# Attention stages with small heads: three stack buffers, stacks made in the third key tile, maxima in the first three key tiles, and maxima that alternate the 64-row halves

## The chip, the core and the metric

The kernel runs on one core of a Trainium2 chip. The metric is the device time of one execution in microseconds (us). Engines are named as in the profile: PE (TensorE), its weight loads PEld, DVE (VectorE), ACT (ScalarE), POOL (GpSimd), SP (the engine that issues the DMAs).

## The reference

The reference is a model of nine stages in float32 on x of 4 sequences of 512 tokens with 256 features: a selective-scan block, a mixture of experts, attention with rotary positions, experts, a gated pair of attentions ("pattern" and "latent"), experts, grouped attention, experts. The change is in three of the attentions, all softmax attention over 512 keys with very small heads:

```
# rotary (16 heads of width 16), queries and keys turned and normalised
logits = einsum('bhqd,bhkd->bhqk', qn, kn) / sqrt(16)
att = softmax(logits);  a = einsum('bhqk,bhkd->bhqd', att, v);  out = a @ Wo + bo
# pattern (16 heads of width 16), out is scaled by a gate
p_scores = einsum('bhqd,bhkd->bhqk', pq, pk) * 16 ** -0.5
# grouped (4 query groups x 8 heads of width 8, keys and values shared by the 4)
scores = einsum('bsqhd,bthd->bqhst', qh, kh) * scale
```

Every query row's maximum is subtracted before the exponential, as in the usual softmax.

## The kernel before

The stages run one after the other, and each of the three has a `Heads` object that writes one list of events. All engines walk this one list in its order and execute their share of it; semaphores order them against each other. So the list sets the order on every engine.

The unit of work is a group: four heads of one sequence. Rotary and pattern have 16 groups each (four to a sequence), grouped has 32 (eight to a sequence). In a group the keys come in four tiles of 128 (`kt` 0 to 3). For each key tile and each of its four heads PE makes a score matmul (event "s", 128 keys x 512 queries, line 1090), ACT takes its exponential into `probs` (line 1126), and PE multiplies probabilities and values in four matmuls of 32 columns each (event "pv", line 1096). The "pv" of a key tile stands after the four scores of the next one. The scores use three PSUM banks, so the score n waits for the exponential n - 3.

While group g runs, group g + 1 is prepared:

- Stacks ("ek", "eq", lines 1077 and 1078): a selection matrix times the high and the low half of projected keys or queries; ACT copies the result out as `k_stack` (line 1111) and `q_stack` (line 1115). In rotary and pattern a stack tile holds two heads, each in 64 of the 128 rows, and a group has two key and two query stacks. In grouped a group has one query stack (32 rows to a head), and the keys stand alone in `k_alone` (zeroes in the rows of the other heads), made once for eight groups. The stacks of g + 2 are made in group g and have two buffers.
- Maxima ("mx", line 1081 on PE, line 1149 on DVE): 16 for a group (four heads, four tiles of 128 queries). PE makes the scores of 128 queries against 512 keys, DVE reduces them to one column of `max_cols`. A maximum needs the stacks of its group.
- Bias (line 1086 on PE, line 1155 on DVE): four small matmuls turn the columns of maxima, DVE adds them to a row of `q_stack`. The first score of a group waits for it. Rotary and pattern have two (tiles 0 and 1), grouped has one.
- Norm ("norm", lines 1160 to 1171 on DVE): divides the sums of the group before, in the second key tile.

Each key tile has three slots in which prepared work stands: slots 0, 3, 6, 9 between its scores 0, 1 and 2 (half of a slot's events after score 0, half after score 1), slots 1, 4, 7, 10 the same around scores 2 and 3, slots 2, 5, 8, 11 after "pv". `schedule` (line 991) puts one maximum in slot 0, then 3, 3, 2, 2, 2 and 3 in slots 1, 3, 4, 6, 7 and 9, so the key tiles get 4, 5, 4 and 3. The bias of tile 0 stands in slot 5, the last bias in slot 10 (after the maxima of the fourth key tile), the stacks of g + 2 in slot 11, the last one of the group. In these slots stand as well the projections of the next sequence (means, "qk", "v", rotation), the normalisation of x, and the output projection ("out") of the last one; in rotary POOL cuts the turned heads of the next sequence into halves ("heads") in slot 3 of a sequence's third group and slot 6 of its fourth.

Everything on PE that is not a score or "pv" shares four PSUM banks in turn (`AUXB`, line 928): such an event waits until the reader (DVE or ACT) of the fourth event before it is done (`free`, line 1034).

## Time and profile before

| | us |
|---|---|
| median of three runs | 4568.15 |
| lowest, highest | 4564.28, 4572.83 |
| profiled execution, its time | 4568.12 |
| its span | 4566.3 |
| loop over groups: rotary, pattern, grouped | 389, 367, 633 |

The granted TensorE clock is 0.912 of full speed on the mean. A row of the profile gives an engine's busy time; "idle before" is how long the engine stood still before an instruction, and the name behind the arrow is what released it.

### The profile page before, as it was taken

How to read it: one execution, taken by the hardware profiler on the slowest of the kernel's cores; microseconds unless marked ns; L12 is line 12 of the kernel's file. 1: busy time of each engine (PE TensorE's matmuls, PEld its weight loads, DVE VectorE, ACT ScalarE, POOL GpSimd, SP SyncE). 2: the span in 40 equal slices, each digit the busy share in tenths (PEclk: the TensorE clock that was granted, in tenths of full speed). 3: DMA queues.
4: the chain of work that ended last, by engine and by line, in shares of the span. 5: the costliest groups of instructions: out<-in, count | busy, mean ns of one | idle time of the engine just before them, and what ended most of it. 6: DMA issues, size and time to landing. Idle time of an engine off the chain costs nothing.

```text
span 4566.3 us, 44420 instructions
## 1 busy us (share of the span) xinstructions
PE 3840.6 (84%) x15840; PEld 2548.4 (56%) x15840; DVE 2580.8 (57%) x4324; ACT 1687.5 (37%) x2807; POOL 1353.1 (30%) x1074
## 2 busy tenths in 40 slices
PE   6869778887978883888889887999878888879999
PEld 4647544435844432555555555788744444457887
DVE  5645366654456652678686765433356766655333
ACT  2433256653235540232323223222245555522222
POOL 3234322214320102333323314444322221143442
PEclk8989889988989976999999998999989999979999
DMA  1010000001000002101000101000000000010000
GB/s 56 1 37 5 29 1 1 1 1 41 1 22 5 5 5 80 28 16 26 18 24 17 26 16 58 18 27 9 16 1 1 1 1 1 1 58 21 25 13 19
DMA packets 32760, 83.27 MB, mean 18 GB/s; under 512 B 6304, under 2 KB 7456, under 8 KB 32288
## 3 DMA queue, kind: packets, MB, share of 16 engines
q1 hardware_dynamic: 32544, 80.44, 5.7%
q8 instruction: 130, 2.13, 0.2%
q14 instruction: 86, 0.70, 0.0%
HBM read 59.44 MB, written 4.19 MB: 14 GB/s over the span
## 4 chain that ended last, share of the span: by engine, by line
PE 54%; DVE 22%; ACT 5%; POOL 3%; issue 2%; DMA 1%; SPq 1%; DVEq 0%; POOLq 0%; ACTq 0%
PE ps L226 11%; PE ps L227 10%; PE ps L228 10%; DVE max_cols L1149 7%; PE ps L1096 5%; PE ps L1935 3%; PE ps L1090 2%; PE ps L296 2%; DVE q_lo L2112 2%; DVE max_cols L2128 2%; PE ps L1081 2%; ACT probs L1126 1%; PE ps L1086 1%; PE ps L800 1%; PE ps L1077 1%
## 5 line engine op out<-in xcount | busy, mean ns | idle before, releaser
L1149 DVE TENSOR_REDUCE max_cols<-ps 128x1 fp32r<-128x512 f32 x1024 | 635.6, 680 | 284.9 <-PE ps L1081 284.1
L1126 ACT ACTIVATE probs<-ps 128x512 f32<-128x512 f32 x1024 | 546.1, 603 | 256.5 <-PE ps L1090 164.6
L754 POOL TENSOR_TENSOR h_lo<-h,h_hi 128x512 fp32r<-128x512 f32 x304 | 392.5, 1291 | 816.6 <-ACT h_hi L834 816.6
L911 DVE TENSOR_TENSOR gated<-silu,ps 128x512 f32<-128x512 f32 x288 | 197.9, 687 | 689.1 <-PE ps L228 665.7
L828 ACT ACTIVATE silu<-ps 128x512 f32<-128x512 f32 x304 | 181.9, 598 | 928.0 <-PE ps L228 927.9
L226 PE MATMUL ps<-xn_hi,w_hi 128*128 128x512 f32 x1216 | 479.5, 394 | 0.0
L227 PE MATMUL ps<-xn_lo,w_hi 128*128 128x512 f32 x1216 | 476.0, 391 | 0.0
L228 PE MATMUL ps<-xn_hi,w_lo 128*128 128x512 f32 x1216 | 475.8, 391 | 0.0
L1096 PE MATMUL ps<-probs,v_aug 128*32 128x512 f32 x2048 | 310.3, 683 | 0.0
L330 POOL CAST o_hi<-o_scaled 128x512 fp32r<-128x512 f32 x64 | 39.1, 612 | 910.1 <-DVE o_scaled L1171 910.1
L1935 PE MATMUL ps<-probs,v_tok 128*128 128x512 f32 x512 | 263.5, 611 | 2.7 <-ACT denominators L1997 2.7
L226 PEld LDWEIGHTS ps<-xn_hi,w_hi 128*128 128x128 f32 x1216 | 231.0, 190 | 49.8 <-issue 1.0
L227 PEld LDWEIGHTS ps<-xn_lo,w_hi 128*128 128x128 f32 x1216 | 230.4, 189 | 49.6 <-issue 1.4
L228 PEld LDWEIGHTS ps<-xn_hi,w_lo 128*128 128x128 f32 x1216 | 230.0, 189 | 48.6
L226 PE MATMUL ps<-h_hi,w_hi 128*128 128x512 f32 x608 | 249.4, 410 | 1.2 <-POOL h_lo L754 1.2
L1090 PE MATMUL ps<-q_stack,k_alone 128*128 128x512 f32 x512 | 213.9, 440 | 31.3 <-ACT probs L1126 29.1
L227 PE MATMUL ps<-h_lo,w_hi 128*128 128x512 f32 x608 | 239.7, 394 | 0.0
L228 PE MATMUL ps<-h_hi,w_lo 128*128 128x512 f32 x608 | 239.6, 394 | 0.0
L1090 PE MATMUL ps<-q_stack,k_stack 64*128 64x512 f32 x512 | 198.8, 485 | 43.3 <-ACT probs L1126 41.2
L1987 ACT ACTIVATE probs<-ps 128x1024 f32<-128x1024 f32 x128 | 131.2, 1025 | 279.1 <-PE ps L1932 278.9
L1081 PE MATMUL ps<-k_alone,q_stack 128*128 128x512 f32 x512 | 201.7, 432 | 37.8 <-ACT q_stack L1115 23.7
L2128 DVE TENSOR_REDUCE max_cols<-ps 128x1 fp32r<-128x512 f32 x256 | 169.2, 682 | 89.6 <-PE ps L1921 89.3
(460 smaller groups left out, 7896.1 us busy)
## 6 DMA issues: line engine op xcount, KB each, us to landing
raw<-in_w_ffn SPq DMA_DIRECT2D x76, 448.0 KB, 3.3
raw<-raw SPq DMA_DIRECT2D x256, 64.0 KB, 2.0
composed_inputs<-in_m_latent SPq DMA_DIRECT2D x1, 5120.0 KB, 15.5
raw<-in_w_mamba SPq DMA_DIRECT2D x8, 448.0 KB, 5.9
raw<-in_w_latent SPq DMA_DIRECT2D x5, 448.0 KB, 16.8
x<-in_x SPq DMA_DIRECT2D x4, 512.0 KB, 6.2
gated_pattern<-gated SPq DMA_DIRECT2D x4, 512.0 KB, 3.1
raw<-gated_pattern SPq DMA_DIRECT2D x4, 512.0 KB, 4.3
```

What stands on the lines that cost most here:

```text
L226: nc.tensor.matmul(psum, wh, xh, start=start, stop=False)
L227: nc.tensor.matmul(psum, wh, xl, start=False, stop=False)
L228: return nc.tensor.matmul(psum, wl, xh, start=False, stop=stop)
L754: nc.gpsimd.tensor_tensor(HL[:, b % 3, :], hb[:, b % 2, :], HH[:, b % 3, :].bitcast(F32), ALU.subtract).then_inc(G.sem, G.step((s, ev)))
L911: nc.vector.tensor_tensor(ga if routed(i) else hb[:, i % 2, :], sg[:, i % 2, :], bank[2 + i % 2], ALU.mult).then_inc(V.sem, V.step((s, "ga ...
L1081: last = nc.tensor.matmul(self.psum(ev), self.q_rows(g, h)[:, q * P:(q + 1) * P], self.k_rows(g, h), start=True, stop=True)
L1090: last = nc.tensor.matmul(self.scores(self.step_no(g, kt, h)), self.k_rows(g, h)[:, kt * P:(kt + 1) * P], self.q_rows(g, h), start=True, s ...
L1096: last = nc.tensor.matmul(bank[6][32 * h:32 * h + 32, :], self.VA[:, (g // self.G4) % 2, kt, self.khead((g % self.G4) * 4 + h), :], self.P ...
L1126: nc.scalar.activation(self.PB[:, n % 8, :], self.scores(n), ACT.Exp, scale=self.scale).then_inc(A.sem, A.step((s, ("exp", n))))
L1149: nc.vector.tensor_reduce(self.MB[:, self.tile_of(g, h) % 2, q, col:col + 1], self.psum(ev), op=ALU.max, axis=AX.X, negate=True).then_inc( ...
L1935: last = nc.tensor.matmul(bank[6 + i], VT[:, (g // HP) % 2, kt, 64 - 64 * i:192 - 64 * i], PB[:, (g * QT + kt) % 2, i, :], start=kt == 0, ...
L2128: nc.vector.tensor_reduce(MB[:, q, 32 * i:32 * i + 1], bank[slot(ev)], op=ALU.max, axis=AX.X, negate=True).then_inc(V.sem, V.step((s, ev)))
```

## The change

- `q_stack` and `k_stack` get three buffers, indexed by g % 3.
- The stacks of g + 2 stand in slot 8 (after "pv" of the third key tile) and no longer in slot 11.
- The maxima of g + 1 are dealt by a table, in halves of a key tile: 2, 2 | 4, 2 | 4, 2 | 0, 0. The key tiles get 4, 6, 6 and 0.
- In rotary and pattern all maxima of a half stand between its two scores, and of each pair of heads the one in the upper 64 rows comes first. The list then reads lower, upper, lower, upper half ... from score 0 to score 1, and again from score 2 to 3. In grouped half of the maxima stand between the two scores and half behind the second.
- What else is in a slot comes whole after its second score; it is no longer split around it.

The biases stay in slots 5 and 10, "norm" in slot 4.

```diff
+        FIRST_MX = (0, 2, 4, 8, 10, 14, 16, 16, 16)
...
-                self.QS = alloc("q_stack", [P, 2, self.tiles, L], F32R)
-                self.KS = None if k_tiles else alloc("k_stack", [P, 2, self.tiles, L], F32R)
+                self.QS = alloc("q_stack", [P, 3, self.tiles, L], F32R)
+                self.KS = None if k_tiles else alloc("k_stack", [P, 3, self.tiles, L], F32R)
...
             def maxima(self, g):
-                return [("mx", g, t * self.per + i, q) for t in range(self.tiles) for q in range(QT) for i in range(self.per)]
+                turn = range(self.per) if self.k_tiles else (1, 0)
+                return [("mx", g, t * self.per + i, q) for t in range(self.tiles) for q in range(QT) for i in turn]
...
                     if n < self.NG:
-                        mx, had = self.maxima(n), 0
-                        for pos, count in ((0, 1), (1, 3), (3, 3), (4, 2), (6, 2), (7, 2), (9, 3)):
-                            self.slots[g][pos] = mx[had:had + count] + self.slots[g][pos]
-                            had += count
...
                     if g + 2 < self.NG:
-                        self.slots[g][11] = self.stacks(g + 2) + self.slots[g][11]
+                        self.slots[g][8] = self.stacks(g + 2) + self.slots[g][8]
...
-                    for h in range(4):
-                        if n < len(units):
-                            events.append(("s",) + units[n] + (h,))
-                        here = at[h // 2]
-                        events += here[len(here) // 2:] if h % 2 else here[:len(here) // 2]
+                    for k in range(2) if n < len(units) else ():
+                        g, kt = units[n]
+                        one, two = (("s", g, kt, h) for h in (2 * k, 2 * k + 1))
+                        mx = self.maxima(g + 1)[FIRST_MX[2 * kt + k]:FIRST_MX[2 * kt + k + 1]] if g + 1 < self.NG else []
+                        if self.k_tiles:
+                            events += [one] + mx[:len(mx) // 2] + [two] + mx[len(mx) // 2:] + at[k]
+                        else:
+                            events += [one] + mx + [two] + at[k]
```

PE in the pattern stage, before, from the fourth key tile of its fourteenth group to the start of the next group (q_stack<- and k_stack operands side by side are scores in line 1090 and maxima in line 1081; 1086 is the bias, 1096 "pv", 1077 and 1078 the stacks):

```order
L1090 MATMUL ps<-q_stack,k_stack 128x512
L1081 MATMUL ps<-k_stack,q_stack 128x512
L1090 MATMUL ps<-q_stack,k_stack 128x512
L1081 MATMUL ps<-k_stack,q_stack 128x512 x2
L1090 MATMUL ps<-q_stack,k_stack 128x512 x2
L1086 MATMUL ps<-h_pattern_hi,max_cols 128x128 x4
L1096 MATMUL ps<-probs,v_aug 32x512 x4
L1077 MATMUL ps<-heads_hi,h_pattern_hi 128x512
L1078 MATMUL ps<-heads_lo,h_pattern_hi 128x512
...
L1090 MATMUL ps<-q_stack,k_stack 128x512 x2
L1081 MATMUL ps<-k_stack,q_stack 128x512
```

PE at the same place now (each line number is one higher), from the third key tile to the start of the next group:

```order
L1091 MATMUL ps<-q_stack,k_stack 128x512 x2
L1082 MATMUL ps<-k_stack,q_stack 128x512 x2
L1091 MATMUL ps<-q_stack,k_stack 128x512
L1097 MATMUL ps<-probs,v_aug 32x512 x4
L1078 MATMUL ps<-heads_hi,h_pattern_hi 128x512
L1079 MATMUL ps<-heads_lo,h_pattern_hi 128x512
...
L1091 MATMUL ps<-q_stack,k_stack 128x512 x4
L1087 MATMUL ps<-h_pattern_hi,max_cols 128x128 x4
L1097 MATMUL ps<-probs,v_aug 32x512 x4
L1091 MATMUL ps<-q_stack,k_stack 128x512
L1082 MATMUL ps<-k_stack,q_stack 128x512 x2
```

The stacks stood between the last "pv" of a group and the next group's first score; now they stand before the four scores of the fourth key tile, and the maxima of that key tile are gone from it.

PE in the grouped stage, before, from the fourth key tile of a plain group to the next group's first scores:

```order
L1090 MATMUL ps<-q_stack,k_alone 128x512
L1081 MATMUL ps<-k_alone,q_stack 128x512
L1090 MATMUL ps<-q_stack,k_alone 128x512
L1081 MATMUL ps<-k_alone,q_stack 128x512 x2
L1090 MATMUL ps<-q_stack,k_alone 128x512 x2
L1086 MATMUL ps<-h_grouped_hi,max_cols 128x128 x4
L1096 MATMUL ps<-probs,v_aug 32x512 x4
L1077 MATMUL ps<-heads_hi,h_grouped_hi 128x512
L1078 MATMUL ps<-heads_lo,h_grouped_hi 128x512
L1090 MATMUL ps<-q_stack,k_alone 128x512 x2
```

PE at the same place now, from the "pv" in the third key tile to the next group's first maximum:

```order
L1097 MATMUL ps<-probs,v_aug 32x512 x4
L1078 MATMUL ps<-heads_hi,h_grouped_hi 128x512
L1079 MATMUL ps<-heads_lo,h_grouped_hi 128x512
L1091 MATMUL ps<-q_stack,k_alone 128x512 x4
L1087 MATMUL ps<-h_grouped_hi,max_cols 128x128 x4
L1097 MATMUL ps<-probs,v_aug 32x512 x4
L1091 MATMUL ps<-q_stack,k_alone 128x512
L1082 MATMUL ps<-k_alone,q_stack 128x512
```

The four scores of the fourth key tile now follow each other with no maximum between them, and the one stack stands ahead of them.

## Rows read from the trace of the kernel before

**Rows 1.** The profile's first part: busy time, share of the span, instructions.
```profile
PE 3840.6 (84%) x15840; PEld 2548.4 (56%) x15840; DVE 2580.8 (57%) x4324; ACT 1687.5 (37%) x2807; POOL 1353.1 (30%) x1074
```

**Rows 2.** Loops: us, busy PE, PEld, DVE, ACT, POOL, PEclk, DMA, GB/s.
```profile
616.00:1005.00 389.00, 332.60 (x1501) 162.23 (x1500) 259.71 (x433) 239.16 (x421) 84.23 (x76) 0.92 0.00 1
1331.00:1698.00 367.00, 312.92 (x1482) 153.64 (x1481) 227.45 (x381) 196.41 (x367) 38.62 (x36) 0.89 0.01 5
3354.00:3987.00 633.00, 534.25 (x2457) 274.61 (x2455) 428.80 (x722) 354.97 (x651) 126.75 (x111) 0.94 0.00 1
```

**Rows 3.** Waits of DVE, rotary, pattern, grouped loop: us, times, longest.
```profile
DVE max_cols L1149 <- PE ps L1081: 66.9, 28, 5.4
...
DVE max_cols L1149 <- PE ps L1081: 67.9, 23, 4.8
...
DVE max_cols L1149 <- PE ps L1081: 129.3, 77, 8.1
DVE q_stack L1155 <- PE ps L1086: 25.0, 28, 4.0
```

**Rows 4.** DVE, timeline, pattern: start, us, operation, [idle before it and what ended it].
```profile
1638.48 0.69 DVE L1155 TENSOR_TENSOR q_stack<-q_stack,ps 128x512 fp32r<-128x512 f32 x1 [0.75 <-PE ps L1086]
1642.21 2.57 DVE L1149 TENSOR_REDUCE max_cols<-ps 128x1 fp32r<-128x512 f32 x4 [3.04 <-PE ps L1081]
...
1657.87 1.89 DVE L1149 TENSOR_REDUCE max_cols<-ps 128x1 fp32r<-128x512 f32 x3 [1.17 <-PE ps L1081]
...
1666.41 2.48 DVE L1149 TENSOR_REDUCE max_cols<-ps 128x1 fp32r<-128x512 f32 x4 [4.76 <-PE ps L1081]
```

**Rows 5.** Timeline of PE, pattern stage, one group's end and the next one's start.
```profile
1637.78 0.66 PE L1086 MATMUL ps<-h_pattern_hi,max_cols 128*128 128x128 f32 x4 [1.03 <-DVE max_cols L1149]
1638.38 1.06 PE L1096 MATMUL ps<-probs,v_aug 128*32 128x512 f32 x8
1639.37 0.50 PE L1077 MATMUL ps<-heads_hi,h_pattern_hi 128*128 128x512 f32 x1
...
1642.92 0.50 PE L1090 MATMUL ps<-q_stack,k_stack 64*128 64x512 f32 x1 [0.51 <-ACT probs L1126]
...
1655.14 1.93 PE L1096 MATMUL ps<-probs,v_aug 128*32 128x512 f32 x8
```

**Rows 6.** Timeline of ACT over the same boundary.
```profile
1640.14 0.69 ACT L1111 ACTIVATE k_stack<-ps,c 128x512 fp32r<-128x512 f32 x1 [2.48 <-PE ps L1078]
...
1642.25 2.08 ACT L1126 ACTIVATE probs<-ps 128x512 f32<-128x512 f32 x4
```

**Rows 7.** Timeline of DVE, grouped stage, first maxima of three groups.
```profile
3507.98 0.69 DVE L1149 TENSOR_REDUCE max_cols<-ps 128x1 fp32r<-128x512 f32 x1 [7.80 <-PE ps L1081]
...
3713.18 2.48 DVE L1149 TENSOR_REDUCE max_cols<-ps 128x1 fp32r<-128x512 f32 x4 [1.12 <-PE ps L1081]
...
3731.18 2.48 DVE L1149 TENSOR_REDUCE max_cols<-ps 128x1 fp32r<-128x512 f32 x4 [2.15 <-PE ps L1081]
```

**Rows 8.** Timeline of PE and ACT, grouped stage, one boundary.
```profile
3727.64 0.66 PE L1086 MATMUL ps<-h_grouped_hi,max_cols 128*128 128x128 f32 x4 [1.38 <-DVE max_cols L1149]
...
3729.23 0.51 PE L1077 MATMUL ps<-heads_hi,h_grouped_hi 128*128 128x512 f32 x1
...
3730.49 2.06 ACT L1126 ACTIVATE probs<-ps 128x512 f32<-128x512 f32 x4
```

**Rows 9.** Busy time by stretch, pattern stage, same columns as group 2.
```profile
1655.00:1664.00 9.00, 8.47 (x31) 3.54 (x31) 4.27 (x7) 2.09 (x5) 0.76 (x1) 0.50 0.01 2
```

**Rows 10.** Timeline of PE, rotary stage: one score and one maximum matmul.
```profile
735.95 0.50 PE L1090 MATMUL ps<-q_stack,k_stack 64*128 64x512 f32 x1
735.95 0.49 PE L1081 MATMUL ps<-k_stack,q_stack 64*128 64x512 f32 x1
```

**Rows 11.** Timeline of POOL and PE, rotary stage, the third group of a batch.
```profile
684.15 1.28 POOL L332 TENSOR_TENSOR heads_lo<-rotated,heads_hi 128x512 fp32r<-128x512 f32 x1
...
688.24 1.06 PE L1096 MATMUL ps<-probs,v_aug 128*32 128x512 f32 x8
```

More of the change, by code:

```diff
@@ L980, in k_rows @@
                     return self.KZ[:, (g // self.G4) % 2, self.khead((g % self.G4) * 4 + h), :]
-                return self.KS[r, g % 2, h // self.per, :]
+                return self.KS[r, g % 3, h // self.per, :]
             def q_rows(self, g, h):
                 r = slice((h % self.per) * self.rows, (h % self.per + 1) * self.rows)
-                return self.QS[:, g % 2, h // self.per, :] if self.k_tiles else self.QS[r, g % 2, h // self.per, :]
+                return self.QS[:, g % 3, h // self.per, :] if self.k_tiles else self.QS[r, g % 3, h // self.per, :]
             def k_tile_no(self, g, h):
@@ L1109, in act @@
                         r = slice(i * self.rows, (i + 1) * self.rows) if self.k_tiles else slice(0, P)
-                        to = self.KZ[r, (g // self.G4) % 2, t * self.per + i, :] if self.k_tiles else self.KS[:, g % 2, t, :]
+                        to = self.KZ[r, (g // self.G4) % 2, t * self.per + i, :] if self.k_tiles else self.KS[:, g % 3, t, :]
                         nc.scalar.activation(to, self.psum(ev)[r, :], ACT.Identity, bias=self.one[r, :]).then_inc(A.sem, A.step((s, ev)))
@@ L1114, in act @@
                     act.wait_ge(PE.sem, PE.at((s, ev)))
-                    nc.scalar.activation(self.QS[:, g % 2, t, :], self.psum(ev), ACT.Copy).then_inc(A.sem, A.step((s, ev)))
+                    nc.scalar.activation(self.QS[:, g % 3, t, :], self.psum(ev), ACT.Copy).then_inc(A.sem, A.step((s, ev)))
                 elif kind == "v":
@@ L1152, in vec @@
                     g, t = ev[1:]
-                    q = self.QS[:, g % 2, t, :]
+                    q = self.QS[:, g % 3, t, :]
                     dve.wait_ge(PE.sem, PE.at((s, ev)))
```

## The prediction

> **What bounds the kernel now.** I read the profile from coarse to fine: the busy shares, the stretches of the three loops that the change touches, the waits of DVE in each of them, then the timelines around one end of a group.
>
> No engine is full. PE is busy for 84% of the span and DVE for 57% [rows 1]. In the loops DVE works 260 of 389, 227 of 367 and 429 of 633 us, so it stands still for 129, 140 and 204 us [rows 2]. What it stands still for is mostly the first maximum of something: 66.9, 67.9 and 129.3 us before line 1149, each time waiting for PE [rows 3]. Two thirds of busy time on an engine, with waits in one place, is the picture of a chain that goes from engine to engine. The timelines show it.
>
> In pattern the last maximum of a group ends, PE makes the bias matmuls, having waited 1.03 us for DVE [rows 5], and DVE adds the bias after 0.75 us [rows 4]. Then PE does "pv", which takes 1.0 us to the start of the stacks, and the eight stack matmuls [rows 5], ACT copies the four stacks out in 2.1 us [rows 6], and only behind this stands the first maximum of the next group: DVE has waited 3.04 us in one group and 4.76 us in the next [rows 4]. In the second of them PE was at half its clock: the same "pv" takes 1.93 us and not 1.06 [rows 5], and the stretch has a granted clock of 0.50, which is 1.2 GHz [rows 9]. In grouped the same wait is 2.15 us with one stack in it, 7.80 us where the keys of the next sequence are stacked as well, and 1.12 us where no stack came between [rows 7]; PE itself waits 1.38 us for the last maximum before the bias [rows 8].
>
> So once in a group first PE waits for DVE's queue of maxima, and then DVE waits for PE and ACT to make stacks. The change puts the stacks over the queue.
>
> **The sum, by DVE's waits.** DVE's own work is the same before and after (as many maxima, adds and norms; a third buffer costs SBUF and no time). So I price the change by what DVE stands still for in a group.
>
> *The gap after the last bias.* Rotary and pattern have 14 ends of a group each in which stacks are made and maxima follow, 28 in all. The gap is 3.9 us, the mean of the 3.04 and the 4.76 [rows 4]; 28 of them are 109 us of the 134.8 us [rows 3]. With the stacks gone from it, it is the one without a stack, 1.12 us [rows 7]. Saved: 2.8 us each, 78 us.
>
> *The new wait before the last bias.* The fourth key tile has no maxima now. From the last maximum's matmul PE has to do: the second score beside it, 0.2 (an estimate, under half of a matmul's 0.50 [rows 10], since matmuls overlap), "pv" 1.0, stacks and scores up to the last score 3.55 (1639.37 to 1642.92, in which that score waits for ACT's copies and first exponential), to the bias 0.3 and the bias 0.66 [rows 5]. That is 5.7 us. DVE has work for a part of it: PE can be at most four maxima ahead, since they share four banks, and four take 2.48 us [rows 4]. DVE waits 3.2 us where it waits 0.75 now [rows 4], 2.5 us more. 28 of them are 70 us, so of the 78 only 8 are left. This is the core of my forecast: most of the wait is not removed but moved to the other side of the bias.
>
> *What fills the new wait.* In the first group of each later sequence (3 in rotary, 3 in pattern) the normalisation of x stands in slot 9, in the fourth key tile: by the code two multiplies and one or two transposes on DVE, at about 0.7 us each like the add of the bias [rows 4] some 2.5 us. It now runs in the new wait: 6 x 2.5 = 15 us.
>
> *The late maxima.* In the fourth key tile DVE waits for PE to hand it the last three maxima, 1.17 us in the group shown [rows 4]. Of the 134.8 us [rows 3] 26 are not in the gaps; I take half, 13 us, for this and count it as saved, because in the second and third key tile the maxima come four at a time and DVE has a queue.
>
> Rotary and pattern together: 8 + 15 + 13 = 36 us.
>
> *Grouped.* 28 plain ends: the gap goes from 2.15 to 1.12 us [rows 7], 1.0 saved. The path before the bias: 0.2 + 1.0 + 1.9 (stack at 3729.23, ACT's exponentials from 3730.49, the first 0.6 long [rows 8]) + 0.3 + 0.66 = 4.1 us less 2.48 of queue is 1.6, and 0.75 now: 0.8 lost. Left: 28 x 0.2 = 6 us. At the three ends with key stacks (7.80 us [rows 7]) the extra 5.65 us of ACT copies moves in front of the bias whole: saved 3 x 6.7 = 20, lost 3 x (4.1 + 5.65 - 2.48 - 0.75) = 3 x 6.5 = 20, nothing left. The rest of the 129.3 us is 129.3 - 28 x 2.15 - 3 x 7.8 = 46 us; a quarter, 11 us, for late maxima (the queue is thinner here, the three maxima were spread between scores), and 2 us for the normalisation in slot 9. Grouped: 19 us.
>
> Sum: 36 + 19 = 55 us. PE's own wait before the bias (1.03 and 1.38 us [rows 5, 8]) isn't counted beside it: it is the same end of a group seen from PE, while DVE works.
>
> *Edits at nothing.* Slot 4 holds the norm and now six maxima share its key tile: DVE gets behind, PE stops at a bank of the four, and the score behind it waits too. That costs nothing while DVE is what is waited for, and it is why I take nothing for PE's waits there; between none and what the slower rival below takes. Rotary's stacks now come one key tile earlier and could wait for POOL's cut of the heads. In the third group of a sequence the cut ends at 685.43 (684.15 + 1.28), and slot 8 begins at the end of the "pv" at 689.24 [rows 11]: 3.8 us to spare, at three places; if the cover were gone it would cost at most some us each. Whole slots behind the second score in place of halves move an event by a matmul or two: nothing, from -3 to +3 us.
>
> *The halves.* A score and a maximum in opposite halves of rows start together at 735.95 [rows 10], so the array runs both. Counting runs of alternating halves, two to a place, a group takes 5 + 5 + 4 + 4 = 18 places before and 4 + 5 + 5 + 2 = 16 now. Two places of at most 0.5 us in 31 groups bound it at 31 us; none excludes zero. I take zero, since in the key tiles where the pairs gain PE then waits for a bank that DVE has not read. The Trainium skill, "TensorEngine Tiling (Array Packing)", section "PSUM Bottleneck", says the same from the other side: tiles speed up TensorE but not the reading of PSUM, which may become the bottleneck. By that rule the halves give 0, by PE alone up to 31 us.
>
> The profiled execution took 4568.12 us (1.8 over its span), the median is 4568.15, so no correction: 4568.1 - 55 = **4513 us**.
>
> **Rivals.**
>
> *A. The wait only moves.* The fills and late maxima are my estimates (28 and 13 us); without them 14 us stay, and three or four waits for banks in groups with other work take these. For it: the 78 against the 70. Against: PE's wait for the last maximum does vanish. Time about 4565 us, within 9 us (0.2%, what a measurement of this kernel can tell) of no change.
>
> *B. The gap counts in full.* If PE and ACT and not DVE set the pace in most groups (other work of 3 us and more stands in them, PE is busy 85% [rows 2]), DVE's new wait in the fourth key tile is hidden, and the saving is the gap: 78 in rotary and pattern, 28 + 20 in grouped, 126 us. For it: PE's busy share. Against: much of that is 1.2 GHz time and overlap. Time: 4442 us.
>
> *C. Slower, through the clock.* The second and third key tile are now bound by DVE: six maxima, the norm, a bias, while PE has little and stands at banks. If the granted clock falls there to 1.2 GHz, as in [rows 9] after such waits, PE is slow just when it makes the path to the bias: of the 4.7 us that are PE's own work in it (all but about 1 us of ACT) almost as much again (1.93 for 1.06 [rows 5]), 4.2, less 1.5 that hides behind ACT, and 1.5 in the gap: 4 us an end. The saving is 55 / 59 = 0.9 us an end, so it decides from 14 of 59 ends that are slow and weren't. With 20: 80 - 55, 4593 us. The clock is 0.92, 0.89 and 0.94 now [rows 2]; it needs to fall by 0.05 or so. The Trainium skill, "TensorE: Matmul & The Clock Gate", Part 1, has the clock follow how busy PE has been of late; the trace agrees as far as it goes (0.50 in [rows 9]).
>
> *D. The halves do what they can.* It adds up to 31 us to my forecast: 4482 us, inside my range.
>
> **How the numbers follow.** Forecast with D 0.56 (its own range 4480 to 4552), B 0.17, A 0.14, C 0.13. Faster by over 0.2%: 0.56 + 0.17 and a little of A, 0.74; within 0.2%: 0.14; slower: 0.12. The range goes from B's 4442 to just before A's far side, 4566.
>
> **What would show it.** After the last bias DVE's wait is 1.1 us in all three stages; before the last bias it is about 3 us in rotary and pattern and 1.6 in grouped, over 6 where keys are stacked. PE's wait for DVE before line 1087 is near zero, and new waits of PE before line 1082 for DVE appear in the second and third key tile. The granted clock of the loops stays within 0.03. I am wrong if the wait before the bias is far below 3 us (then B), if the clock falls (C), or if the loops save under 10 us together although the gap is 1.1 us (A).

## The result, and the profile after

| | before | after |
|---|---|---|
| median of five runs each, us | 4568.15 | 4587.12 |
| lowest to highest | 4564.28 to 4572.83 | 4579.73 to 4594.83 |
| profiled execution, its span | 4568.12, 4566.3 | 4579.73, 4577.9 |
| mean granted clock | 0.912 | 0.910 |

The ratio is 1.0039, with a 95% interval of 1.0023 to 1.0055. The change makes the kernel 19 us slower. I forecast 4513 us, 55 us faster, with a range from 4442 to 4566 us; the result is outside it.

The first part of the page hardly moves (after; as [rows 1]):

```profile
PE 3847.8 (84%) x15840; PEld 2554.4 (56%) x15840; DVE 2572.9 (56%) x4324; ACT 1699.4 (37%) x2807; POOL 1353.5 (30%) x1074
```

The loops say where the time went. To compare like with like I cut each from its first "pv" to its last. Columns as in [rows 2]; rotary, pattern, grouped. Before:

```profile
625.00:1021.00 396.00, 340.01 (x1532) 163.01 (x1535) 257.67 (x431) 242.18 (x429) 86.12 (x78) 0.91 0.00 1
1337.00:1699.00 362.00, 308.74 (x1467) 151.53 (x1470) 222.89 (x374) 193.02 (x360) 38.62 (x36) 0.89 0.01 5
3364.00:3988.00 624.00, 525.39 (x2434) 269.19 (x2437) 421.58 (x711) 349.86 (x643) 126.75 (x111) 0.95 0.00 1
```

After:

```profile
626.00:1042.00 416.00, 352.54 (x1530) 166.36 (x1526) 253.63 (x429) 245.68 (x428) 86.08 (x78) 0.87 0.00 1
1357.00:1713.00 356.00, 304.54 (x1466) 149.60 (x1468) 220.44 (x373) 196.05 (x359) 38.55 (x36) 0.90 0.01 5
3376.00:4003.00 627.00, 525.78 (x2434) 272.27 (x2436) 420.36 (x710) 353.01 (x642) 126.89 (x111) 0.94 0.00 1
```

Rotary is 20 us longer (21 to a tenth: 395.4 and 416.3), pattern 6 shorter, grouped 3 longer. DVE's busy time in each is 1 to 4 us shorter than before, so what was added is waiting. The three loops together are 18 us longer, everything outside them 6 us shorter, which gives the 11.6 us between the two profiled executions. The medians are 19 us apart.

DVE around the last bias (after; line 1156 is its bias add, 1150 its maxima): rotary, pattern twice, the grouped group in which keys are stacked, and a plain grouped one.

```profile
903.75 0.69 DVE L1156 TENSOR_TENSOR q_stack<-q_stack,ps 128x512 fp32r<-128x512 f32 x1 [3.75 <-PE ps L1087]
...
1640.23 0.69 DVE L1156 TENSOR_TENSOR q_stack<-q_stack,ps 128x512 fp32r<-128x512 f32 x1 [6.51 <-PE ps L1087]
...
1662.31 0.69 DVE L1156 TENSOR_TENSOR q_stack<-q_stack,ps 128x512 fp32r<-128x512 f32 x1 [1.43 <-PE ps L1087]
1663.77 2.48 DVE L1150 TENSOR_REDUCE max_cols<-ps 128x1 fp32r<-128x512 f32 x4 [0.77 <-PE ps L1082]
...
3519.91 0.69 DVE L1156 TENSOR_TENSOR q_stack<-q_stack,ps 128x512 fp32r<-128x512 f32 x1 [9.06 <-PE ps L1087]
...
3747.07 0.69 DVE L1156 TENSOR_TENSOR q_stack<-q_stack,ps 128x512 fp32r<-128x512 f32 x1 [1.99 <-PE ps L1087]
3748.72 2.48 DVE L1150 TENSOR_REDUCE max_cols<-ps 128x1 fp32r<-128x512 f32 x4 [0.96 <-PE ps L1082]
```

The wait after the bias, 3.04 and 4.76 us before [rows 4], is 0.77; the wait ahead of it, 0.75 before, is 1.4 to 6.5 in these rows, and 9 where keys are stacked. The stacks have carried their wait to the other side of the bias. (Before, the longest wait ahead of a bias was 1.2 us in rotary and pattern and 4.0 us in grouped.)

Now everything else that DVE waits for. Waits of DVE (us in total, times, longest) in the rotary loop, before:

```profile
DVE max_cols L1149 <- PE ps L1081: 62.3, 26, 5.4
...
DVE z L1429 <- PE ps L1295: 14.4, 12, 3.2
DVE x L1439 <- PE ps L228: 13.1, 6, 3.8
DVE q_stack L1155 <- PE ps L1086: 10.2, 13, 1.1
```

and after:

```profile
DVE q_stack L1156 <- PE ps L1087: 55.9, 12, 8.6
DVE z L1430 <- PE ps L1296: 26.5, 12, 4.4
DVE x L1440 <- PE ps L228: 23.1, 6, 6.5
...
DVE max_cols L1150 <- PE ps L1082: 12.3, 8, 3.7
```

The maxima wait 50.0 us less, the bias 45.7 us more. The reads of the next sequence's rotation (`z`) and of the last one's output projection (`x`) wait 12.1 and 10.0 us more. These four rows give 18 of the 21 us. In pattern it is the same: maxima 54.5 less, bias 28.9 more, and `heads_lo` and `gated` 24.4 more:

```profile
DVE q_stack L1156 <- PE ps L1087: 39.3, 13, 6.5
DVE heads_lo L1616 <- ACT heads_hi L1567: 37.8, 12, 5.0
DVE gated L1622 <- PE ps L228: 23.8, 6, 5.7
DVE max_cols L1150 <- PE ps L1082: 10.4, 12, 1.9
```

(before, the same stretch of the loop:)

```profile
DVE max_cols L1149 <- PE ps L1081: 64.9, 22, 4.8
DVE heads_lo L1615 <- ACT heads_hi L1566: 21.7, 11, 2.5
DVE gated L1621 <- PE ps L228: 15.5, 6, 3.8
DVE q_stack L1155 <- PE ps L1086: 10.4, 13, 1.2
```

One place shows how. DVE after, in a rotary group; the `z` transposes read what PE makes in the slots of the other work:

```profile
895.80 1.28 DVE L1150 TENSOR_REDUCE max_cols<-ps 128x1 fp32r<-128x512 f32 x2
899.28 0.72 DVE L1430 STREAM_TRANSPOSE z<-ps 128x512 f32<-128x512 f32 x1 [2.21 <-PE ps L1296]
903.75 0.69 DVE L1156 TENSOR_TENSOR q_stack<-q_stack,ps 128x512 fp32r<-128x512 f32 x1 [3.75 <-PE ps L1087]
```

Its last two maxima end at 897.08. Then PE makes four stacks and the rotation's matmuls, DVE waits 2.21 us for them, does 0.72 us of work, and waits 3.75 us more. The edit writes `self.stacks(g + 2) + self.slots[g][8]`, so the eight stack matmuls stand ahead of everything else in slot 8. PE at this place, after (1078 is a stack matmul, 1296 the one that `z` reads):

```profile
896.26 0.50 PE L1078 MATMUL ps<-heads_hi,h_rotary_hi 128*128 128x512 f32 x1
...
898.22 1.02 PE L1296 MATMUL ps<-raw,c 128*128 128x512 f32 x2
```

So the stacks take 1.96 us of PE in front of it. The same `z` read before the change, when no stack stood there:

```profile
883.12 0.72 DVE L1429 STREAM_TRANSPOSE z<-ps 128x512 f32<-128x512 f32 x1 [0.31 <-PE ps L1295]
```

In grouped the two waits of the core alone are DVE's balance (before 127.4 and 23.8 in this stretch; after, here):

```profile
DVE q_stack L1156 <- PE ps L1087: 77.4, 28, 9.1
DVE max_cols L1150 <- PE ps L1082: 70.1, 60, 3.4
```

57.3 saved and 53.6 lost.

### The profile page after: what moved, and what is told of

Its sections match the earlier page's. It is cut to its first block, busy times and chain, and to the rows that moved or that the text cites. A ratio compares the mean times of both kernels' runs of the same rounds, so it can differ in the third digit from the quotient of the medians.

```text
span 4577.9 us, 44488 instructions
## 1 busy us (share of the span) xinstructions
PE 3847.8 (84%) x15840; PEld 2554.4 (56%) x15840; DVE 2572.9 (56%) x4324; ACT 1699.4 (37%) x2807; POOL 1353.5 (30%) x1074
## 4 chain that ended last, share of the span: by engine, by line
PE 56%; DVE 20%; ACT 5%; POOL 3%; issue 2%; DMA 1%; SPq 1%; DVEq 0%; POOLq 0%; ACTq 0%
PE ps L226 10%; PE ps L227 10%; PE ps L228 10%; PE ps L1097 5%; DVE max_cols L1150 5%; PE ps L1091 3%; PE ps L1082 3%; PE ps L1936 3%; PE ps L296 2%; DVE max_cols L2129 2%; DVE q_lo L2113 2%; ACT probs L1127 1%; PE ps L800 1%; PE ps L1078 1%; PE ps L1922 1%
## 5 line engine op out<-in xcount | busy, mean ns | idle before, releaser
L1150 DVE TENSOR_REDUCE max_cols<-ps 128x1 fp32r<-128x512 f32 x1024 | 629.5, 679 | 124.2 <-PE ps L1082 118.2
L1127 ACT ACTIVATE probs<-ps 128x512 f32<-128x512 f32 x1024 | 556.4, 601 | 378.8 <-PE ps L1091 283.2
L1082 PE MATMUL ps<-k_stack,q_stack 64*128 64x512 f32 x512 | 194.5, 488 | 73.0 <-DVE q_stack L1156 42.0
L1082 PE MATMUL ps<-k_alone,q_stack 128*128 128x512 f32 x512 | 205.5, 440 | 50.3 <-DVE max_cols L1150 25.9
```

Of the source, the lines that this page charges most:

```text
L1082: last = nc.tensor.matmul(self.psum(ev), self.q_rows(g, h)[:, q * P:(q + 1) * P], self.k_rows(g, h), start=True, stop=True)
L1127: nc.scalar.activation(self.PB[:, n % 8, :], self.scores(n), ACT.Exp, scale=self.scale).then_inc(A.sem, A.step((s, ("exp", n))))
L1150: nc.vector.tensor_reduce(self.MB[:, self.tile_of(g, h) % 2, q, col:col + 1], self.psum(ev), op=ALU.max, axis=AX.X, negate=True).then_inc( ...
```

## The experiments

Two theories stood from the start. In the first, DVE's order costs the time: the maxima are bunched in the first three key tiles and the fourth is empty. In the second, the granted clock costs it: the order lets PE stand still at places after which it gets 1.2 GHz. Each kernel was timed in five rounds against the kernel before. The table holds what all of them gave; a loop's product of time and clock counts each us at half speed as half a us. The clock is the mean over forty equal stretches of the loop. The product is a diagnostic, not a law: a wait for an engine other than PE does not get shorter with PE's clock.

| kernel | ratio to before, 95% | rotary: us, clock, product | pattern | grouped |
|---|---|---|---|---|
| before | | 395, .909, 359 | 362, .887, 321 | 624, .945, 590 |
| after | 1.0039, 1.0023 to 1.0055 | 416, .874, 364 | 356, .905, 322 | 626, .937, 587 |
| e1_stacks_only | 0.9985, 0.9970 to 0.9999 | 411, .875, 360 | 366, .873, 319 | 600, .949, 569 |
| e2_maxima_only | 1.0075, 1.0052 to 1.0098 | 411, .888, 365 | 364, .878, 320 | 641, .933, 598 |
| e3_rotary_as_before | 1.0012, 0.9994 to 1.0030 | 392, .918, 360 | 352, .918, 323 | 630, .932, 587 |
| e4_maxima_even | 1.0052, 1.0033 to 1.0071 | 408, .885, 361 | 365, .882, 322 | 624, .926, 578 |
| e5_stage_mix | 0.9943, 0.9929 to 0.9958 | 396, .912, 361 | 356, .905, 322 | 600, .949, 570 |
| e6_after_filled | 1.0036, 1.0022 to 1.0051 | 406, .928, 376 | 351, .928, 325 | 626, .937, 587 |
| e7_before_filled | 1.0003, 0.9990 to 1.0016 | 398, .919, 366 | 348, .946, 329 | 624, .943, 588 |
| e8_halves_and_whole_slots | 1.0105, 1.0090 to 1.0121 | 399, .911, 363 | 368, .873, 321 | 661, .914, 604 |
| e9_dealt_as_before | 0.9979, 0.9969 to 0.9990 | 404, .882, 356 | 349, .926, 323 | 603, .953, 575 |
| e10_mix_and_fill | 0.9934, 0.9921 to 0.9947 | 389, .929, 362 | 346, .951, 329 | 600, .949, 569 |
| e11_grouped_middle | 0.9969, 0.9957 to 0.9980 | 389, .930, 362 | 358, .900, 322 | 600, .963, 578 |

How far one trace can be trusted: where the same order stands in several kernels, its loop took 389 to 396 us (rotary as before, five traces), 352 to 358 (pattern as after, four), 626 to 630 (grouped as after, three), 600 each (grouped with before's dealing and slot 8, three). So 4 us either way are scatter.

**e1_stacks_only.** The kernel before, with three buffers and the stacks in slot 8.

```diff
-                self.QS = alloc("q_stack", [P, 2, self.tiles, L], F32R)
+                self.QS = alloc("q_stack", [P, 3, self.tiles, L], F32R)
...
-                        self.slots[g][11] = self.stacks(g + 2) + self.slots[g][11]
+                        self.slots[g][8] = self.stacks(g + 2) + self.slots[g][8]
```

> The kernel before with three stack buffers and the stacks in slot 8; the maxima stay at 4, 5, 4 and 3 to the key tiles, and slots are split in halves as before. Theory 1 (the dealing of the maxima, which leaves none in the fourth key tile, costs what the stacks' new place saves): faster than before, 4530 to 4550 us, with DVE's gap after the last bias near 1.1 us and its wait before the last bias under 1.5 us in most groups. Theory 2 (the stacks' new place itself costs, by ACT's copies standing before the fourth key tile's exponentials): 4568 us or more. Theory 3 (the granted clock is the cause and not a sign): the clock of the rotary loop decides whatever the order, 0.87 and about 4585 us if it falls, 0.91 and below 4568 us if not.

Measured: 4563.27 us, between the expectations: grouped saves 24 us, as the first theory has it; rotary loses 16 with its clock at 0.875, as the second and third have it; pattern loses 4, which is scatter. Waits of DVE in the grouped loop:

```profile
DVE max_cols L1149 <- PE ps L1081: 98.7, 80, 3.9
DVE q_stack L1155 <- PE ps L1086: 25.2, 27, 2.9
```

The maxima wait 28.7 us less than before and the bias only 1.4 us more (127.4 and 23.8 in the same stretch). With maxima still in the fourth key tile DVE has something to do while PE makes the stack, and the wait doesn't move but goes. In grouped this is what my forecast hoped for, and the stacks alone bring it.

In rotary and pattern e1 shows something else. Its maxima stand where they stood before, yet the reads that I found lengthened in the kernel after are as long here:

```profile
DVE x L1439 <- PE ps L228: 24.1, 6, 7.0
DVE z L1429 <- PE ps L1295: 21.0, 12, 2.2
...
DVE heads_lo L1615 <- ACT heads_hi L1566: 38.7, 12, 5.0
DVE gated L1621 <- PE ps L228: 23.4, 6, 5.8
```

There are 36 such reads in the two loops, and 18 of them stand in slot 8 (6 `z`, 3 `x`, 6 `heads_lo`, 3 `gated`). Their waits, added up over the timelines, in us:

| | before | e1 | e9 | e4 | after | e2 | e8 |
|---|---|---|---|---|---|---|---|
| stacks in slot | 11 | 8 | 8 | 8 | 8 | 11 | 11 |
| maxima to the key tiles | 4, 5, 4, 3 | 4, 5, 4, 3 | 4, 5, 4, 3 | 4, 4, 4, 4 | 4, 6, 6, 0 | 4, 6, 6, 0 | 4, 4, 4, 4 |
| the 18 reads in slot 8 | 26.5 | 68.9 | 66.4 | 66.2 | 79.0 | 39.4 | 25.4 |
| all 36 reads | 64.8 | 107.1 | 98.1 | 102.5 | 111.2 | 82.8 | 62.7 |

So it is mainly the stacks in front of these reads that lengthen them, 42 us with no maximum moved. Moving the maxima away adds about 10 to it (e1 and after), or 13 where the stacks stay in slot 11 (before and e2).

**e2_maxima_only.** The kernel after, with the stacks back in slot 11.

```diff
-                        self.slots[g][8] = self.stacks(g + 2) + self.slots[g][8]
+                        self.slots[g][11] = self.stacks(g + 2) + self.slots[g][11]
```

> The kernel after with the stacks back in slot 11; maxima dealt 4, 6, 6 and 0. Theory 1: slower than both kernels, 4600 us or more, since the wait of about 4 us behind the last bias is back and the empty fourth key tile stays. Theory 2: near or below before, about 4560 us.

Measured: 4603.43 us; grouped 641. Its waits there:

```profile
DVE max_cols L1150 <- PE ps L1082: 118.4, 64, 8.1
DVE q_stack L1156 <- PE ps L1087: 47.1, 28, 3.9
```

Bias 23 us more than before, maxima 9 less. The new dealing costs 17 us in grouped with the stacks in slot 11, and 26 with them in slot 8 (626 against e1's 600). In both pairs the half-slots differ too; e9 takes these out.

**e3_rotary_as_before.** The kernel after, with rotary's list as before (`self.old`: before's dealing and half-slots, stacks in slot 11).

```diff
+        OLD = (C_ROT,)
...
+                        if self.old:
+                            mx, had = self.maxima(n), 0
+                            for pos, count in ((0, 1), (1, 3), (3, 3), (4, 2), (6, 2), (7, 2), (9, 3)):
...
-                        self.slots[g][8] = self.stacks(g + 2) + self.slots[g][8]
+                        at_ = 11 if self.old else 8
+                        self.slots[g][at_] = self.stacks(g + 2) + self.slots[g][at_]
```

> The kernel after, but rotary keeps the order of before (its buffers are three). The traces put the loss of the change into rotary (its loop 404 us before, 424 after), with 4 us won in pattern and 4 lost in grouped. If that holds, this kernel takes 4568 minus 4 plus 4 minus about 3 between the stages, 4560 to 4570 us. If the loss of rotary comes from something outside its order (a placement of buffers, a clock that falls anyway), it stays at 4585 us.

Measured: 4575.16 us, rotary 392. That is above the 4560 to 4570 us expected, and by its ratio (1.0012) it can't be told from before. (The expectation cuts the rotary loop elsewhere; by the cut used here its 404 and 424 us are 395 and 416.) The loss is rotary's, and the stages can be changed apart from each other.

**e4_maxima_even.** The kernel after with four maxima in each key tile.

```diff
-        FIRST_MX = (0, 2, 4, 8, 10, 14, 16, 16, 16)
+        FIRST_MX = (0, 2, 4, 6, 8, 10, 12, 14, 16)
```

> The kernel after with the maxima dealt evenly, 4, 4, 4 and 4 to the key tiles, everything else as in it (stacks in slot 8, halves alternating, slots whole). Theory 1: the best so far, 4510 to 4545 us, since DVE has maxima queued while PE makes stacks and rotations, and the bias follows them closely. Theory 2: no better than after, 4585 us. If the whole slots behind the second score are what costs, also about 4585 us.

Measured: 4588.96 us, grouped 624, where 4510 to 4545 us were expected. Filling the fourth key tile to its end is no cure. The bias wait goes back (25.6 us), but now PE waits for the last maximum. Waits of PE in the grouped loop, e4:

```profile
PE ps L1087 <- DVE max_cols L1150: 45.1, 31, 3.7
```

and e1, whose last maxima stand behind score 1 and so two scores ahead of the bias:

```profile
PE ps L1086 <- DVE max_cols L1149: 23.1, 25, 1.4
```

So there is a best place for the last maxima, between the two ends. The first theory in its simple form (the more evenly dealt, the better) fell.

**e5_stage_mix.** Each stage in its best list so far: rotary as before, pattern as after, grouped with before's dealing and half-slots and stacks in slot 8.

```diff
+        OLD = (C_ROT, C_GRP)
...
+                        at_ = 11 if self.old and not self.k_tiles else 8
+                        self.slots[g][at_] = self.stacks(g + 2) + self.slots[g][at_]
```

> Rotary in the order of before, pattern in the order of after, grouped with the stacks in slot 8 but its maxima and slots as before. The stages are independent if the traces are read rightly: rotary 395, pattern 352 to 356, grouped 600 us against 395, 362 and 624 before, so 4568 - 0 - 8 - 24 = about 4536 us. If instead the loops' times only scatter with the granted clock and no order is better than another, it comes out at 4560 to 4575 us.

Measured: 4539.92 us; the three loops came as in the kernels that they are taken from, within 1 us.

**e6_after_filled.** The kernel after, with one score and one maximum of each rotary and pattern group written four times into the same bank: six matmuls more in a group, the same values.

```diff
+                    again = 4 if not self.k_tiles and ev == self.maxima(g)[12] else 1
+                    for _ in range(again):
...
+                    again = 4 if not self.k_tiles and (kt, h) == (3, 2) else 1
+                    for _ in range(again):
```

> The kernel after; in rotary and pattern the third score of the fourth key tile and the thirteenth maximum of a group are made four times over into the same bank (six more matmuls a group, the same values), at places where PE is about to wait. Theory 3 (half-clock time is the cause of rotary's loss): the mean clock of the rotary loop rises from 0.874 to 0.91 or more and the loop shortens by 8 us or more from 416 us although PE does some 20 us more work. Theory 1 (the waits themselves cost, and the clock only follows): the loop takes 416 us or more. Pattern likewise, from 356 us.

Measured: 4581.53 us. The loops (rotary, pattern):

```profile
628.00:1034.00 406.00, 351.45 (x1628) 175.91 (x1627) 254.22 (x429) 246.12 (x429) 86.08 (x78) 0.93 0.00 1
1351.00:1702.00 351.00, 313.06 (x1557) 164.56 (x1559) 220.61 (x372) 195.04 (x359) 38.57 (x36) 0.93 0.01 5
```

With 96 matmuls more the rotary loop takes 10.8 us less, PE's busy time is 1 us shorter, and the clock goes from 0.87 to 0.93. More work is not faster by itself, so this trace puts a part of rotary's time to the clock, as the second theory has it: about half of the 21 us come back. The timed runs don't confirm it: the ratios to before are 1.0036 and 1.0039, with overlapping intervals. The gain and its size rest on one trace. The order of the waits stays as after (bias 55.2, `z` 25.5, `x` 22.8 us).

**e7_before_filled.** The same with the kernel before (scores 2 of the first and 3 of the fourth key tile, four times).

```diff
+                    again = 4 if not self.k_tiles and (kt, h) in ((0, 2), (3, 3)) else 1
+                    for _ in range(again):
```

> The kernel before; in rotary and pattern the third score of the first key tile and the last score of the fourth are made four times over into the same bank, before the waits for ACT's exponential and for the last maximum. Theory 3: clock of rotary from 0.909 and of pattern from 0.887 up by 0.02 or more and both loops 4 us or more shorter (395 and 362 us now). Otherwise the loops stay or grow by up to 10 us each.

Measured: 4570.61 us. Rotary, pattern:

```profile
630.00:1028.00 398.00, 353.56 (x1624) 179.50 (x1620) 258.19 (x430) 242.79 (x428) 86.02 (x78) 0.92 0.00 1
1347.00:1695.00 348.00, 308.66 (x1558) 160.54 (x1562) 223.25 (x373) 192.42 (x359) 38.55 (x36) 0.95 0.01 5
```

Pattern is 14 us shorter at a clock of 0.95, rotary not shorter: its clock was 0.91 and had little to give. The timed ratio (1.0003) shows no gain of the whole; the pattern's rests on this trace, taken of one of the faster runs, and on e10's.

**e8_halves_and_whole_slots.** e4 with the stacks in slot 11: of the change, mainly the alternating halves and the whole slots are left.

```diff
-        FIRST_MX = (0, 2, 4, 8, 10, 14, 16, 16, 16)
+        FIRST_MX = (0, 2, 4, 6, 8, 10, 12, 14, 16)
...
-                        self.slots[g][8] = self.stacks(g + 2) + self.slots[g][8]
+                        self.slots[g][11] = self.stacks(g + 2) + self.slots[g][11]
```

> The kernel after with stacks in slot 11 and the maxima dealt 4, 4, 4 and 4: what is left of the change is the alternation of the halves, the whole slots behind the second score, and the third buffer. If the alternation pays, 4555 us or less. If the whole slots cost (the even dealing came to 4589 us where the stacks alone came to 4563), 4585 us or more. If neither matters, 4568 us, and the two parts of the change only hurt together.

Measured: 4614.97 us, the slowest. Rotary (399) and pattern (368) are about as before; the loss is in grouped:

```profile
3373.00:4034.00 661.00, 534.36 (x2431) 277.22 (x2430) 424.36 (x712) 344.78 (x641) 126.76 (x111) 0.91 0.00 1
```

Even dealing with late stacks has both waits: PE waits for the last maximum, then DVE for the stack. The gain of slot 8 over slot 11 at this dealing is 37 us, at before's 24, at after's 15. So the edits don't add, and e8 didn't isolate what it was made for.

**e9_dealt_as_before.** The kernel after with before's counts in each key tile, 4, 5, 4, 3: the halves and whole slots stay.

```diff
-        FIRST_MX = (0, 2, 4, 8, 10, 14, 16, 16, 16)
+        FIRST_MX = (0, 1, 4, 7, 9, 11, 13, 16, 16)
```

> The kernel after with the maxima dealt as before, 1, 3, 3, 2, 2, 2, 3 and 0 to the half key tiles; stacks in slot 8, slots whole behind the second score, upper half first. If the dealing is what costs in grouped (theory 1), its loop takes 595 to 605 us, as with the stacks alone and slots in halves (600), and not 626. If the whole slots cost, it stays at 620 us or more. Rotary stays near 410 us either way, since its stacks stand in slot 8. Whole kernel: 4565 or 4590 us.

Measured: 4551.95 us, below both values expected. Rotary and grouped:

```profile
628.00:1032.00 404.00, 346.84 (x1528) 172.01 (x1527) 256.62 (x430) 242.60 (x426) 86.02 (x78) 0.88 0.00 1
3368.00:3971.00 603.00, 512.28 (x2433) 269.45 (x2429) 422.68 (x710) 345.12 (x642) 126.90 (x111) 0.95 0.00 1
```

One table of numbers turns the whole from 1.0039 to 0.9979, and grouped from 626 to 603 us. Against e1, from which it differs by the halves and whole slots alone, grouped is equal within scatter. Pattern is 17 us shorter (366, 349), but its product is not (319, 323), and the ratios are the same, so this is no gain by places in the array. Rotary stays long (404), as its stacks stand in slot 8.

**e10_mix_and_fill.** e5 with pattern's list as before and e7's repeated scores in pattern alone.

```diff
+        OLD = (C_ROT, C_PAT, C_GRP)
...
+                    again = 4 if self.fill and (kt, h) in ((0, 2), (3, 3)) else 1
```

> Rotary in the order of before, grouped with only the stacks in slot 8, pattern in the order of before with the repeated scores (six more matmuls a group) that raised its clock. Theory 3 and the independence of stages: pattern's loop 348 us at a clock near 0.945, grouped 600, rotary 395; whole kernel 4540 - 8 = about 4530 us. If pattern's 348 us was chance, 4540 us or more.

Measured: 4527.42 us, ratio 0.9934, below before and after. It can't be told from e5 (0.9943): the intervals overlap. Pattern again takes 346 us at 0.95:

```profile
1336.00:1682.00 346.00, 306.82 (x1558) 159.60 (x1554) 223.10 (x373) 192.78 (x359) 38.62 (x36) 0.95 0.01 5
```

**e11_grouped_middle.** e5 with grouped's maxima dealt 4, 5, 5, 2.

```diff
-                            for pos, count in ((0, 1), (1, 3), (3, 3), (4, 2), (6, 2), (7, 2), (9, 3)):
+                            for pos, count in ((0, 1), (1, 3), (3, 3), (4, 2), (6, 3 if self.k_tiles else 2), (7, 2), (9, 2 if self.k_tiles else 3)):
```

> The stage mix (rotary as before, pattern as after) with grouped's maxima dealt 4, 5, 5 and 2. Theory 1, as the runs now leave it: PE's wait before the bias shrinks and DVE's wait there grows as maxima move out of the fourth key tile, with the best somewhere between; grouped's loop within 6 us of 600, against 600 at 4, 5, 4, 3 and 624 at 4, 4, 4, 4. A loop above 610 us would say that the place of single maxima against other work, and not their number in the last key tile, decides.

Measured: 4547.73 us, grouped 600 as with 4, 5, 4, 3. By the traces two or three maxima in the fourth key tile do equally well, and none costs 23 us. The timed runs are less kind to two: the ratio is 0.9969 against e5's 0.9943, and the intervals barely touch.

## Why the prediction was wrong

*The gap after the last bias: right.* I said 3.9 to 1.12 us, saved 78 us in rotary and pattern. The gaps, from the end of the last bias to the first maximum, added up over the timelines, went from 57 to 20 us in rotary and from 55 to 11 in pattern: 81 us. In grouped the maxima wait 57.3 us less, I had 60 with all terms.

*The path from the last maximum to the last bias: this step failed.* I built it from "pv", stacks, scores and bias, 5.7 us, with nothing else in slot 8, and I took DVE's other waits as unchanged without a reason. But in 12 of the 14 groups in which rotary and pattern make stacks, slot 8 holds other work of PE (rotation, projections, "out"), and the eight stack matmuls now stand ahead of it. Where DVE reads that work, it waits for the stacks there: the `z` and `x` reads of rotary wait 22.1 us more, `heads_lo` and `gated` of pattern 24.4. This term of 46.5 us is missing from my sum. In e1, where no maximum has moved, it is 42 us; the rest goes with the maxima that stood beside these reads. Where ACT reads the work (the values, fourth group of a sequence) the wait lands on the bias instead, as no maximum is left ahead of it: 6.5 us in pattern and 6.8 to 8.6 in rotary, where I had 3.2.

*The new wait before the last bias: right in place, too small in size.* I said 70 us less 15 for fills, 55, and it is 45.7 + 28.9 = 75 us. The fill itself came true: at five of the six ends with the normalisation of x in slot 9 the bias waits 0 us. At the others I had 3.2 everywhere, and they are 3.75 us at plain ends of rotary, 0.94 at plain ends of pattern (whose wait stands at `heads_lo`, ahead of it) and over 6 in the fourth groups. In grouped I had 42 and it is 53.6. At ends with key stacks it is 9 us, where I had over 6. The core of the forecast, that the wait moves to the other side of the bias, is what the trace shows.

*"The late maxima", 13 + 11 us saved: true as a wait, wrong as time.* In rotary and pattern the maxima wait 104.5 us less, 77 of it right at the end of the gaps, 27 elsewhere, more than my 13. It comes back at the bias and at the other reads. So rotary and pattern come out as -104.5 + 74.6 + 46.5, with 5 us of smaller rows and 6.5 us less work on DVE 15 us longer, where I had 36 shorter. In grouped the choice between dealing the maxima 4, 5, 4, 3 and 4, 6, 6, 0 is worth 23 us (e9 and after), and early stacks save 24 us where the former dealing stays (e1). They cancel: that is why grouped stands at 626 for 624, where I had 19 us saved.

*DVE's waits as the price: not enough in rotary and pattern.* A loop is DVE's work and its waits, so that account always closes; but how long it waits for PE hangs on PE's clock too, and I took that as given. The product of time and clock stays at 356 to 365 us in rotary in all eleven lists without repeated matmuls there, and at 319 to 323 in the ten such lists of pattern. Over these orders the loops' times differ mostly in how much of them runs at 1.2 GHz. In rotary this is 2 x (1 - 0.909) x 395 = 72 us before and 105 after; by this estimate half speed costs up to half of the 33, some 17 of the 21 us. Repeated matmuls raised the clock in the traces of e6 (rotary) and e7 (pattern), and those loops got shorter. The Trainium skill, "TensorE: Matmul & The Clock Gate", section "A second HAM failure mode: psum-queue depth-cycling", has a kernel in which short idle times between groups of matmuls let the clock swing between its two levels; e6 agrees as far as it goes, with 0.874 going to 0.928 for six matmuls more in a group. In grouped the product moves by 35 us with the order (569 to 604), and there DVE's waits were the better price.

*Edits at nothing.* Whole slots and alternating halves: nothing in grouped (600, 603) and none that the ratios show elsewhere. PE's waits for DVE in the second and third key tile came as foretold (25.9 us in grouped before line 1082), and cost nothing that I could set apart. POOL's cut of the heads, for which I had 3.8 us to spare in the third group of a sequence, held PE up in the fourth, which I had not looked at (rotary loop, after):

```profile
PE ps L1302 <- POOL heads_hi L330: 5.3, 3, 1.8
```

There ACT's copies of the stacks stand behind its own work on what POOL makes (ACT waits 3.30 us for it at 720.45), and PE waits for a bank that ACT has not read.

*The rivals.* A was the nearest in its mechanism: the wait moves and the small terms that I added are not there. It had no term for the other work and gave 4565. C gave 4593 with a chance of 0.13, the time nearest to the measured 4587, but that is partly luck. It named the clock, which fell by 0.035 in rotary, more than the 0.03 that I allowed, rose in pattern and fell by 0.008 in grouped. Its cause was six maxima to a key tile, and that is not it: e1 and e9 deal 4, 5, 4 and 3, and their rotary clock is 0.875 and 0.882. B and D are out: no hidden wait, no gain by halves.

*What stays open.* Why rotary's clock falls. All four lists with its stacks in slot 8 (after, e1, e4, e9) have it at 0.874 to 0.885, and the lists of before in slot 11 at 0.909 to 0.930; but e2 has 0.888 with slot 11 and e8 0.911. So it isn't the slot alone. PE's own waits did change places: before, it stood 14.2 us at the last maxima, after, it stands before the next group's first maxima, waiting for DVE's late bias (rotary loop, after):

```profile
PE ps L1082 <- DVE q_stack L1156: 16.9, 10, 2.4
PE ps L1082 <- DVE raw L1424: 9.0, 10, 0.9
```

But this can't be the whole cause: in e1 PE waits 14.2 us at the last maxima and 5.1 us for the late bias, both as before, and the clock is 0.875 all the same. Nor is it shown why the product should be nearly constant, or how the longer path through slot 8 and the clock share rotary's 21 us: the `z` and `x` waits were read at the clock that they happened at.

## What to carry to other kernels

When a piece of work is moved, list what stands behind its new place and now waits for it, as carefully as what gets free at the old one; in this kernel the reads behind the moved stacks waited 42 us longer by that alone. Work that an engine can do at any time is worth most beside the longest serial path: here two or three of sixteen maxima, ending a little before the step that needs them. Where the second engine has no queue left, earlier production only moves its wait. And before pricing an order by one engine's waits, multiply each stage's time by its granted clock: if the product hardly changes between orders, look at how much of the stage runs at half speed before trying another order.

## What the runs showed of the hardware

- With matmuls repeated into the same bank, six in a group and 96 in a loop, the traced loop was shorter where the clock was low: rotary 416 to 406 us (0.874 to 0.928), pattern 362 to 348 (0.887 to 0.946). Where it was 0.909 they gave nothing (395, 398). The timed runs of the whole kernel show no gain that is clear of noise: 1.0039 without and 1.0036 with them (after, e6), 1.0003 for e7 against before, 0.9943 and 0.9934 (e5, e10).
- Eight matmuls put ahead of another one on PE (1.96 us of its time at full clock) showed as 1.9 us more of DVE's wait for the `z` read in slot 8 (0.31 to 2.17 us in e1, 2.21 after).
- Two kernels whose orders differ only in details can differ by 17 us in a loop (pattern in e1 and e9: 366 us at 0.873 and 349 at 0.926) while the product of time and clock differs by 4.
- A score and a maximum in opposite halves of the rows do start together, but alternating them over a group changed no loop's product by more than 4 us (e1 and e9, rotary 360 and 356, pattern 319 and 323).
